# A context that the host also lays out by columns: read as such in the wide attention stage and for the keys of layer 1

## What is computed

```python
# layer 1, cross attention: 16 heads of 16 features. The first 256 features of
# the context are keys as they are, the last 256 are values as they are
# (the loads of this stage in the kernel show it); x gives queries and
# 128 more keys and values.
q, k, v = x @ wq, x @ wk, x @ wv
keys, values = concat(context[..., :256], k), concat(context[..., 256:], v)
x = layernorm(x + softmax(q keys^T / 4) values @ w_proj + b_proj)

# layer 2, cross attention: 16 heads of 64 features (the "wide" stage)
kv = einsum('bmc,cf->bmf', context, Wkv)        # 512 -> 2048
k, v = split(kv, 2); q = einsum('bnd,df->bnf', x, Wq) * 64 ** -0.5
# one learned null key and value is put in front of k and v
out = softmax(q k^T) v @ Wout                   # 1024 -> 256
x = layernorm(x + layernorm(out) * ln_scale + ln_bias)
```

## Time and profile before

| | |
|---|---|
| median of 3 runs | 3257.7 us (3253.26 to 3266.2) |
| the profiled execution | 3258.44 us |
| its span, first to last instruction | 3256.6 us |
| mean granted TensorE clock | 0.917 of full |
| layer 1 stage with context | about 912 to 1205 us of the span |
| wide stage | about 1942 to 2420 us |

### The profile page before, as it was taken

The page is one execution under the profiler, slowest core; times in us unless marked ns, Lnnn a source line. Parts: engine busy times, 40 slices in busy tenths (PEclk is TensorE's granted clock), DMA queues, the critical chain, the costliest instruction groups (busy, mean ns, idle before and its releaser), DMA issues. The chain is left out here.

```text
span 3256.6 us, 71154 instructions
## 1 busy us (share of the span) xinstructions
PE 2778.4 (85%) x25095; PEld 2167.2 (67%) x25153; DVE 1647.6 (51%) x3584; ACT 1453.7 (45%) x4618; POOL 1387.8 (43%) x1626
## 2 busy tenths in 40 slices
PE   5888888658979978969984979999994995989989
PEld 5777777446656656755654757887773674767878
DVE  3888899673446654561125763333332223554633
ACT  4555565244446656743335862333330334762310
POOL 2656667452346665543334651322331222662311
PEclk9999999679989989979996989999995997999999
DMA  2000000100010000051120011000006111002010
GB/s 78 2 2 2 2 2 2 50 18 28 1 32 17 16 19 1 0 185 43 46 74 31 0 44 55 10 10 10 6 1 252 31 32 49 1 2 69 23 36 20
DMA packets 70793, 106.17 MB, mean 33 GB/s; under 512 B 10768, under 2 KB 48272, under 8 KB 70304
## 3 DMA queue, kind: packets, MB, share of 16 engines
q1 hardware_dynamic: 64608, 86.68, 7.9%
q0 software_dynamic: 5952, 16.26, 1.6%
HBM read 88.50 MB, written 14.42 MB: 32 GB/s over the span
## 5 line engine op out<-in xcount | busy, mean ns | idle before, releaser
L700 POOL TENSOR_TENSOR probs<-probs,inv 128x512 f32<-128x512 f32 x320 | 328.7, 1041 | 303.3 <-DVE inv L1028 302.9
L3497 POOL TENSOR_TENSOR hc<-h,bc 128x1024 f32<-128x1024 f32 x128 | 301.9, 2359 | 181.4 <-DVE h L3764 167.7
L924 ACT ACTIVATE probs<-s_ps,negmax 128x128 f32<-128x128 f32 (+1 forms) x768 | 297.8, 416 | 8.4 <-DVE negmax L988 7.0
L3764 DVE TENSOR_TENSOR_SCAN h<-da,dbu_ps 128x1024 f32<-128x1024 f32 x128 | 292.3, 2284 | 10.3 <-DVE dbu_ps L3776 4.8
L796 PE MATMUL t_ps<-ident,probs 128*128 128x128 f32 x1280 | 210.4, 288 | 52.9 <-POOL probs L700 43.9
L796 PEld LDWEIGHTS t_ps<-ident,probs 128*128 128x128 f32 x1280 | 140.6, 143 | 119.8 <-POOL probs L700 56.4
L3582 PE MATMUL dta_ps<-dt,a_spread 32*128 32x128 f32 x2048 | 161.9, 300 | 45.2 <-ACT da L3710 25.7
L3710 ACT ACTIVATE da<-dta_ps 128x1016 f32<-128x1016 f32 x128 | 130.3, 1018 | 139.7 <-PE dta_ps L3582 139.3
L3776 DVE TENSOR_TENSOR dbu_ps<-dbu_ps,bc 128x1024 f32<-128x1024 f32 x128 | 155.7, 1216 | 69.2 <-PE dbu_ps L3587 68.9
L3582 PEld LDWEIGHTS dta_ps<-dt,a_spread 32*128 32x128 f32 x2048 | 136.3, 202 | 68.2 <-ACT da L3710 30.8
L988 DVE TENSOR_REDUCE negmax<-s_ps 128x4 f32<-128x1024 f32 (+1 forms) x128 | 156.6, 1223 | 46.7 <-PE s_ps L782 44.9
(11 more groups left out here) (509 smaller groups left out, 6933.0 us busy)
## 6 DMA issues: line engine op xcount, KB each, us to landing
c_in<-in_ctx SPq DMA_DIRECT2D x48, 256.0 KB, 2.7
w_up<-in_L_ffn_w SPq DMA_DIRECT2D x8, 1024.0 KB, 12.8
w_down<-in_L_ffn_w SPq DMA_DIRECT2D x8, 1024.0 KB, 11.6
w_gate<-in_L_ffn_w SPq DMA_DIRECT2D x8, 512.0 KB, 9.5
w_up<-in_L_ffn_w SPq DMA_DIRECT2D x8, 512.0 KB, 9.4
w_down<-in_L_ffn_w SPq DMA_DIRECT2D x8, 512.0 KB, 9.8
w_gate<-expert_rows_out SPq DMA_DIRECT2D x8, 512.0 KB, 7.1
wkv<-in_L_xattn_Wkv SPq DMA_DIRECT2D x2, 2048.0 KB, 12.8
```

The source lines that it names most:

```text
L700: pool.tensor_tensor(probs[:, u % 2, i], probs[:, u % 2, i], inv[:, u % 2, HB * i:HB * (i + 1)].unsqueeze(2).broadcast_to([P, HB, W]), ALU ...
L924: last = act.activation(probs[:, u % 2, i, k, :], src, ACT.Exp, bias=negmax[:, u % 2, at], accum_out=sums[:, u % 2, at])
L3497: pool.tensor_tensor(hc[:, s % 4], h[:, s % 2], bc[:, j, 1, :].unsqueeze(1).broadcast_to([P, 2 * G, P]), ALU.mult).then_inc(hc_ready.sem, 1)
L3764: dve.tensor_tensor_scan(flat(h[:, s % 2]), flat(da[:, s % 4]), dbu_ps[s % 2][:, :, :, :].rearrange("p i g t -> p (i g t)"), 0.0, ALU.mult ...
```

## The change

In the wide stage SP loads `ctx_turned[b]` straight into `cT`; `c_in`, the four transposes and ScalarE's copy are gone. `keys` now waits for the load. `bank_a` has three uses an item in place of four, `bank_b` still four, and the load for item b waits until the values of item b - 2 are made. In layer 1 the key half of the context is loaded from `ctx_turned` straight into `kT`, and only the value half into `c_in`; the two transposes and ScalarE's copy are gone. There are two loads an item instead of one, the first of which waits for the scores of item b - 2, and the first `score` of an item waits for both loads. The host already made `ctx_turned` before.

```diff
 # self_attention_stage, SP
                     for b in range(B):
-                        sp.wait_ge(xT_turned.sem, xT_turned.freed(b))
+                        sp.wait_ge(scored.sem, scored.done(NP * (b - 2) + NP - 1))
+                        sp.dma_start(kT[:, b % 2, :, 0:P], context_turned[b, :, 0:DC, :]).then_inc(c_landed[b % 2].sem, 16)
                         sp.wait_ge(c_used.sem, c_used.freed(b))
-                        sp.dma_start(c_in[:, b % 2, :], context[b]).then_inc(c_landed[b % 2].sem, 16)
+                        sp.dma_start(c_in[:, b % 2, :], context[b, :, D:CTX]).then_inc(c_landed[b % 2].sem, 16)
...
 # turn, and score for u == 0, on TensorE
-                    if context is not None:
-                        pe.wait_ge(c_landed[j].sem, landed_at(b, j))
...
-                    if context is not None:
-                        for qc in range(DC):
-                            last = pe.transpose(bank_a[:, DC + qc, :], c_in[:, j, qc * P:(qc + 1) * P], core.ident[:, :])
...
+                        if context is not None:
+                            pe.wait_ge(c_landed[j].sem, landed_at(b, j))
...
 # copy_turned on ScalarE
-                    if context is not None:
-                        act.wait_ge(scored.sem, scored.done(NP * (b - 2) + NP - 1))
-                        act.activation(kT[:, j, :, 0:P], bank_a[:, DC:, :], ACT.Copy)
...
 # wide_context_stage, SP
-                    sp.wait_ge(a_made.sem, a_made.done(use(b - 2, TURN)))
-                    sp.dma_start(c_in[:, b % 2, :], context[b]).then_inc(landed[b % 2].sem, 16)
+                    sp.wait_ge(b_made.sem, b_made.done(use(b_made, b - 2, "values")))
+                    sp.dma_start(cT[:, b % 2], context_turned[b]).then_inc(landed[b % 2].sem, 16)
...
 # turn and keys on TensorE
-                    pe.wait_ge(landed[j].sem, landed_at(b, j))
-                    claim(bank_a, a_taken, b, TURN)
-                    for cc in range(CC):
-                        last = pe.transpose(bank_a[:, cc, :], c_in[:, j, cc * P:(cc + 1) * P], core.ident[:, :])
-                    last.then_inc(a_made.sem, 1)
...
-                    pe.wait_ge(a_taken.sem, a_taken.done(use(b, TURN)))
+                    pe.wait_ge(landed[j].sem, landed_at(b, j))
+                    claim(a_taken, b, "keys")
...
 # ScalarE
-                def take_turned(b, j):
-                    act.wait_ge(a_made.sem, a_made.done(use(b, TURN)))
-                    act.wait_ge(b_made.sem, b_made.done(use(b - 2, VALUES)))
-                    act.activation(cT[:, j], bank_a[:, :, :], ACT.Copy).then_inc(a_taken.sem, 1)
```

More of the change, by code:

```diff
@@ L620, in landed_at @@
         def landed_at(b, j):
[L621 removed]
+            return c_landed[j].base + 16 * (b - j) + 32
         def every_item(eng, unit):
@@ L1467, in masked_context_stage, with wide_context_stage @@
             n.advance(16 * B // 2)
-def wide_context_stage(core, context, wq, wkv, null_kv, wo, ln_scale, ln_bias, head_rows):
+def wide_context_stage(core, context_turned, wq, wkv, null_kv, wo, ln_scale, ln_bias, head_rows):
     nc, loads = core.nc, core.loads
@@ L1529, in wide_context_stage, with use @@
         weights = loads.base + 16 * len(plain)
-        KEYS, VALUES, QUERIES, TURN = 1, 2, 3, 4
-        def use(n, what):
-            return 4 * (n - 1) + what if what == TURN else 4 * n + what
+        A_USES, B_USES = ("keys", "values", "queries"), ("turn", "keys", "values", "queries")
+        def use(taken, n, what):
+            uses = A_USES if taken is a_taken or taken is a_made else B_USES
+            return len(uses) * n + uses.index(what)
         def landed_at(b, j):
@@ L1564, in fetch @@
                 def fetch(b, j):
-                    pool.wait_ge(b_made.sem, b_made.done(use(b - 2, TURN)))
+                    pool.wait_ge(b_made.sem, b_made.done(use(b_made, b - 2, "turn")))
                     pool.tensor_copy(x_in[:, j, :], core.x[:, b, :]).then_inc(x_in_ready.sem, 1)
@@ L1647, in _, with claim @@
             def _(pe):
-                def claim(b_or_a, taken, n, what):
-                    pe.wait_ge(taken.sem, taken.done(use(n, what) - 1))
+                def claim(taken, n, what):
+                    pe.wait_ge(taken.sem, taken.done(use(taken, n, what) - 1))
                 def turn(b, j):
-                    pe.wait_ge(landed[j].sem, landed_at(b, j))
-                    claim(bank_a, a_taken, b, TURN)
-                    for cc in range(CC):
-                        last = pe.transpose(bank_a[:, cc, :], c_in[:, j, cc * P:(cc + 1) * P], core.ident[:, :])
-                    last.then_inc(a_made.sem, 1)
                     pe.wait_ge(x_in_ready.sem, x_in_ready.done(b))
-                    claim(bank_b, b_taken, b, TURN)
+                    claim(b_taken, b, "turn")
                     for cc in range(DC):
@@ L1678, in values @@
                     bank, made, taken = ((bank_a, a_made, a_taken), (bank_b, b_made, b_taken))[half]
-                    claim(bank, taken, b, VALUES)
+                    claim(taken, b, "values")
                     first = INNER + half * INNER // 2
@@ L1687, in queries @@
                     bank, made, taken = ((bank_a, a_made, a_taken), (bank_b, b_made, b_taken))[half]
-                    claim(bank, taken, b, QUERIES)
+                    claim(taken, b, "queries")
                     columns_of(bank, wq_sb, half * INNER // 2, xT[:, j], DC, made)
                 def null_scores(b, j):
-                    pe.wait_ge(b_taken.sem, b_taken.done(use(b, TURN)))
+                    pe.wait_ge(b_taken.sem, b_taken.done(use(b_taken, b, "turn")))
                     pe.wait_ge(null_taken.sem, null_taken.done(b - 1))
@@ L1699, in score @@
                     taken = (a_taken, b_taken)[u]
-                    pe.wait_ge(taken.sem, taken.done(use(b, QUERIES)))
+                    pe.wait_ge(taken.sem, taken.done(use(taken, b, "queries")))
                     pe.wait_ge(exp_done.sem, exp_done.done(2 * b + u - 1))
@@ L1721, in weigh @@
                     taken = (a_taken, b_taken)[u]
-                    pe.wait_ge(taken.sem, taken.done(use(b, VALUES)))
+                    pe.wait_ge(taken.sem, taken.done(use(taken, b, "values")))
                     pe.wait_ge(pT_even.sem, pT_even.done(g))
@@ L1807, in take_values @@
                 def take_values(b, j):
-                    act.wait_ge(a_made.sem, a_made.done(use(b, VALUES)))
+                    act.wait_ge(a_made.sem, a_made.done(use(a_made, b, "values")))
                     act.wait_ge(weighed.sem, weighed.done(2 * (b - 2)))
@@ L1861, in take_turned @@
                 def take_turned(b, j):
-                    dve.wait_ge(b_made.sem, b_made.done(use(b, TURN)))
+                    dve.wait_ge(b_made.sem, b_made.done(use(b_made, b, "turn")))
                     dve.wait_ge(null_made.sem, null_made.done(b - 2))
@@ L1866, in take_keys @@
                 def take_keys(b, j):
-                    dve.wait_ge(b_made.sem, b_made.done(use(b, KEYS)))
+                    dve.wait_ge(b_made.sem, b_made.done(use(b_made, b, "keys")))
                     dve.wait_ge(scored.sem, scored.done(2 * (b - 2) + 1))
@@ L1871, in take_values @@
                 def take_values(b, j):
-                    dve.wait_ge(b_made.sem, b_made.done(use(b, VALUES)))
+                    dve.wait_ge(b_made.sem, b_made.done(use(b_made, b, "values")))
                     dve.wait_ge(weighed.sem, weighed.done(2 * (b - 2) + 1))
@@ L2013, in wide_context_stage @@
             n.advance(2 * B)
-        for n in per_use:
-            n.advance(4 * B)
+        for n in (a_made, a_taken):
+            n.advance(len(A_USES) * B)
+        for n in (b_made, b_taken):
+            n.advance(len(B_USES) * B)
         null_made.advance(B)
```

31 lines of the change are left out of this document (14 added, 17 removed).

## The result

The median is 3242.57 us (3235.02 to 3247.39, 9 runs), against 3257.7 (3250.26 to 3266.2, 9 runs) beside it. The ratio is 0.9951, with a 95% interval of 0.9937 to 0.9965: about 15 us, 0.5%, faster.

What follows compares the result with a forecast made beforehand. TensorE was taken to fill the wide stage; layer 1 was a ScalarE-VectorE loop with TensorE late once an item. Gains 3.5 + 4.5 + 1.6 = 9.6 us off the median 3257.7 gave 3248.1 us, range 3240 to 3257.

Steps and rivals of the forecast that it cites:

- Wide, the mechanism: Wide stage: removed transposes save 0.39 us an item, but only 0.11 at a branch, where the wait for `bank_b_taken` holds TensorE's sequencer.
- `null_scores` on `pnT`: Wide stage: `null_scores` would not wait for `pnT`, ready at 2129.0 against TensorE's arrival at 2129.18.
- Forecast: Main case, chance 0.5: wide-stage items take 29.26 us without a branch and 29.54 with one.
- all of it is gained: Rival, chance 0.2: the wide stage's branch is covered, every item takes 29.26 us, and the kernel 3245 to 3246 us.
- seven such boundaries: Wide stage: seven item boundaries with a branch, six in the loop and one on entering it, each gaining only 0.11 us.
- 7 x 0.39 + 7 x 0.11 = 3.5 us: Wide stage's gain: seven boundaries without a branch at 0.39 us, seven with one at 0.11; bounds 2.7 and 5.4 us.
- 14 x 0.32 = 4.5 us: Layer 1's loop: `project_qk` no longer waits for `xT`, so 14 items gain 0.32 us each; bounds 2.2 and 5.9 us.
- Together 1.6 us: Layer 1's start: `project_qk` 1.15 us earlier, plus 0.44 us for the second turn's two dropped transposes; bounds 0.4 and 2.5.
- The first two pieces: Layer 1's start: TensorE begins 0.45 us earlier, after the last weight lands; `project_qk` moves 1.15 us in all.
- shifts of the clock: Whole kernel: chance 0.07 left for shifts in the clock that hide or double the gain.
- such a shift as a sign: Untouched stages: one changing its granted clock over tens of microseconds would put the prediction wrong by more than its range.
- The slower rival: Layer 1, chance 0.03: GpSimd's value copy waits for its load, queued behind the key load on SP; 3314 us.

Runs made afterwards that it cites:

- e5: The changed kernel with x turned into `bank_a` in place of `bank_b` in the wide stage, branch kept: 3240.85 us, ratio 0.994 to the kernel before.
- e6: The changed kernel with TensorE's loop over the wide stage's items written out, without branch or register work, `bank_b` kept: 3252.26 us in one execution.
- e4: The changed kernel with two transposes, of the identity and read by nobody, put back ahead of those of x in layer 1: 3252.78 us in one execution.
- e3: The changed kernel with ScalarE's copy put back in layer 1, into a tile nobody reads, ahead of the copy to `xT`: 3240.12 us in one execution.
- e2: The changed kernel with the wide stage put back as before, so only layer 1 is changed: 3245.27 us, ratio 0.996 to the kernel before.
- e8: The changed kernel with both ScalarE's copy and the two transposes put back in layer 1, loads still direct: 3250.97 us in one execution.
- e7: The changed kernel with TensorE's first turn of layer 1 waiting for the context again, nothing else put back: 3253.97 us in one execution.
- e9: The changed kernel with copy, two transposes and the first turn's wait for the context put back in layer 1, loads still direct: 3259.66 us in one execution.
- again: The kernel before the change, unchanged, profiled once more: 3258.92 us in that execution.
- e1: The changed kernel with layer 1 put back as before, so only the wide stage is changed: 3255.39 us, ratio 0.9985 to the kernel before.

## Why the prediction was right or wrong

**Wide, the mechanism: right, the count of branches wrong.** Items shorten by less at a branch, the sequencer is why, and e5 and e6 show it by taking away either of its two causes. `null_scores` on `pnT`: no wait, right. Forecast and *all of it is gained* were told apart by the 29.45 against 29.21 us. But the prediction had seven such boundaries, "six times in the loop, and once on entering it, which I treat alike". There were five: the entry cost nothing, and the last branch, where the loop ends, 0.03 us.

**Wide, the size: the term 7 x 0.39 + 7 x 0.11 = 3.5 us was met in part by luck.** Measured is 0.44 without a branch and 0.20 with one, and 4.4 us from the third turn to the last. The first was read as a distance from start to start of weight loads. The trace resolves it: before, the turn's first load and that of `pn` behind it lie 0.605 us apart (2127.56 to 2128.17), after 0.169 (2112.24 to 2112.41), and the difference is 0.436. Within a run of these transposes the second load follows the first by 0.06 us and the others by 0.109; the x transposes take over the short step, so that four of the long ones are saved. At the branch I reckoned the scores 0.80 us behind the turn; they came 2112.96 - 2112.24 = 0.72 behind it. Of the 4.4 us, 3.7 were left in the stage's length, since the stretch behind the last turn is 0.7 us longer, with 24.0 us at 1.2 GHz in place of 21.3. Each of these sizes would have raised the sum to 4 or more; the end of the stage took it down again.

**Layer 1, the items: right.** 14 x 0.32 = 4.5 us was predicted; the two parities give 0.36 and 0.28, which is 0.32 on average, and from the third turn to the last 4.5 us are gained. The chain behind it was argued well in one point and half wrong in another: `xT` does set `project_qk`, but of the 0.32 us the copy isn't the sole owner. With the copy alone gone (e4) only 0.24 is gained, with the transposes alone gone (e3) 0.22.

**Layer 1, the start: the step that failed.** I wrote "Together 1.6 us. Bounds are 0.4 [...] and 2.5". The first two pieces came as reckoned: `project_qk` is 1.36 us earlier (1.15 predicted), and TensorE begins when the last weight lands. But by the third turn 5.4 us were gained. What the sum left out is the granted clock, which rises 10.2 us behind its fall in place of 20.5. TensorE works some ten microseconds at 2.4 GHz that it worked at 1.2 before. I had given shifts of the clock 0.07 and otherwise taken them as scatter around the sum; this one belongs to the change, or at least comes with it every time: 20.5 us in the three profiles with the old layer 1, 10.2 in the seven with the new one and its like (after, e2 to e6, e8), 13.7 (e7) and 17.1 (e9) in the two that wait for the context at the start, one execution each. The whole stage adds up as 5.4 us to the third turn, 4.5 us from there to the last (215.2 us in place of 219.6) and 0.4 behind it: 10.2 with the roundings. Of the 5.4, the work that the prediction counted is 1.6, so the clock is worth near 3.8, an estimate. e8 agrees: with all the work of copy and transposes back its third turn is still 5.3 us earlier than before's, 1.5 of which it has at the first transpose and 3.7 behind it. (Its stage is 7.0 us shorter, not 5.3, since its last 41 us pass with less time at 1.2 GHz than before's last 43.)

**Why the clock rises earlier stays open.** The copy (e3), the transposes (e4) and both (e8) leave the stretch at 10.2 us. e7 is no test of the wait, for the wait cost it nothing. Counted from the stage's first load, TensorE's first transpose and the rise of the clock came at

```
                        first transpose   clock rises
before, again, e1       7.82 7.49 7.26    22.0 21.7 21.4
after, e2 to e6, e8     6.28 to 7.16      11.2 to 11.8
e7                      7.15              12.7
e9                      7.88              18.0
```

e8 and e9 differ by the wait alone: with it the first transpose comes 1.6 us later and the rise 6.3 us later. So a late start of TensorE may carry most of the difference, which is argued from one execution each, and no run delays the start by itself. What remains between e9 and before is the loads (one of 512 columns an item against two of 256), the waits that go with them, and the source and place of the transposes. None of these was separated, and with all of them before's clock rises at 22.0.

**The rest is not the change's.** 10.2 + 3.7 = 13.9 us lie in the two stages. The 18.7 us of the profiled pair differ from that mostly by what the clock does elsewhere: the alibi stage's 200.5 us occur in after alone, and every other kernel has 203.4 to 204.9. The prediction had named such a shift as a sign that it would miss its range; it was 4.3 us and the range held. The 15.1 us of the medians weren't taken apart. The point forecast of 9.6 us was low by the clock's part above all, and the range held because it was wide.

**The slower rival** didn't occur: no wait of the value copy in the loop, and the key load, which stands ahead of it in SP's queue, holds nothing up.

**The price of a branch.** The prediction weighed the Trainium skill ("Advanced Engine Details and Errata", Control Flow Timing), which gives about 108 ns for a compare-and-branch. The trace of after doesn't agree for TensorE: 208 ns in the row. The Trainium skill's figure would have put a branched item at 29.65 - 0.22 = 29.43 us as an estimate, nearer to the 29.45 measured than my 29.54, but not for its reason. From the end of the `qT` copy to the scores it took 2112.96 - 2112.02 = 0.94 us where I had reckoned 2128.36 - 2127.34 = 1.02, and the branch kept its length.

## What to carry to other kernels

Removing work from a full engine gains it where the sequencer is ahead, and less where a late semaphore wait stands close before a branch: here such a wait was better put on a bank that had long been free. Count the branches in the trace: entering the loop cost nothing here, and leaving it 0.03 us. Two pieces in one row ahead of a common reader can each look nearly free (0.10 and 0.08 us here) and cost more than their sum once both are there (0.32), so cost them together as well as apart. And look at the granted clock at the start of a stage before reckoning there: here it was worth more (near 3.8 us) than the work that the start dropped (1.6), for a reason that stays open. The lengths of untouched stages must be compared before any difference is given to the edit.

## What the runs showed of the hardware

- A compare-and-branch occupied TensorE's sequencer for 0.208 us in after, and VectorE's for 0.056 us at the same loop end. The last one, where the loop ends, took TensorE's 0.076 us.
- TensorE's sequencer had no row for 0.7 us ahead of a transpose that waited for `qT` (after, 2111.4 to 2112.1), and for 0.1 us where the transpose waited for a bank that was free (e5).
- The stretch at 1.2 GHz at the start of one stage had four lengths, 20.5, 17.1, 13.7 and 10.2 us, in kernels that differ by two transposes, a copy, a wait and the form of a load; it was 20.5 in all three profiles with the old code, and 10.2 in all seven with direct loads and no wait at the start.
- The first stage, the same in all twelve profiles, took 583.8 to 598.7 us, with 82 to 118 us of it at 1.2 GHz. This alone is as large as the effect of the whole change.
